# Four batch inputs of an attention: expert outputs weighted, summed and transposed in one TensorE product

## The chip, the cores and the metric

The kernel runs on one NeuronCore of one Trainium2 chip. Its time is the device time of one launch in microseconds (us), the median of several runs. The engines of a core run their own instruction queues side by side and wait for one another by semaphores: TensorE (PE in the profile), VectorE (DVE), ScalarE (ACT), GpSimd (POOL), and SyncE (SP), which here only issues transfers. ACTq, POOLq and SPq are the transfers that an engine issues.

## The reference

Two layers on x of 4 sequences x 512 tokens x 512 channels. Every sublayer reads its input through a gate (`cond`), a bidirectional recurrence that gives one factor per token and channel, which is multiplied with a sigmoid of x. The first layer is a Mamba-2 block and a mixture of eight experts, the second a causal attention with 16 heads in 4 groups and a gated feed-forward. What the change touches is the end of the experts and the beginning of the attention:

```python
for e in range(E):                       # 8 experts, each token routed to 2
    h = x @ w1[e].T + b1[e]
    y = x_glu * sigmoid(1.702 * x_glu) * (x_lin + 1.0)
    ye = y @ w2[e].T + b2[e]
    we = sum(routing * (top_idx == e))
    out = out + ye * we[:, None]
x = x + out                              # end of the expert sublayer
u = sigmoid(x) * gate                    # input of the attention
k, v, q = u @ w_kv, u @ w_q              # then softmax(q k) v @ w_dense, added to x
```

## The kernel before

Everything is kept transposed: XT holds the 512 channels as 4 chunks of 128 partitions, and the 2048 tokens in the free dimension. Each engine's program is written out by hand in its own block, in the order in which it is to run; nothing is scheduled by a planner. A tensor that TensorE multiplies in the attention is split into a rounded part (`_hi`, a ScalarE copy) and the remainder (`_lo`, a VectorE subtraction), and each product is done as three (`three`, L341 to L343).

The experts run over 39 blocks of 128 gathered tokens. Their results go to `y_dram`, one row per token and chosen expert. After the last block, each batch (sequence) b of 4 has to be brought home. It has 4 blocks of 128 tokens (tb; a = 4b + tb counts all 16):

1. GpSimd (`gather_out`) issues two indirect transfers for a block, one per chosen expert, into `og` (two slots, reused) or, for blocks 2 and 3 of batch 0, into `og2`. From block 4 on, it first waits until the slot's former block has been transposed (`cb_T`).
2. VectorE (`weighted`) multiplies the first by its weight `we`, one number per token and so per partition, and adds the second times its own (`cb_sum`).
3. TensorE (`combine_T`) transposes the sum in 4 pieces into the PSUM bank `CB`.
4. VectorE (`combine`) adds the bank to XT (`cb_done`). There is one bank, so a transpose waits for the add before it.
5. `gated_input` makes the attention's input of the batch in four whole steps of 4 x 512 columns: a tanh on ScalarE, times the gate on VectorE, `u_hi` on ScalarE, `u_lo` on VectorE (`u_split`).

The attention goes over 16 items i (group x batch), with 4 heads h each. TensorE computes in turn keys, query, scores, transposed probabilities, context and the dense product of the item before. Batch 0 is brought home before item 0 (`batch_T(0)`, `batch_input(0)`), batch 1 in the middle of item 0 after the context of head 0, batch 2 at the end of item 0, batch 3 at the end of item 1. ScalarE's `k_hi_copy(0)` also waits for a transfer, because `k_hi` lies where the gate stage has its last values: `act.wait_ge(g_out[LATE], ...)`, the store of the last gate pair to `g_dram` by SyncE (`g_store`, L400). SyncE's queue in this stage is, in order: the gate of batch 0 (`u_g`), the attention weights' first part, a wait for `cb_sum` of 4 blocks, the other two parts, the gates of batches 1 to 3, this store. ScalarE's `att_hi` and VectorE's `att_lo` split the weights. GpSimd ends the last gate pair (`gate_result`, L512 to L516) between the gathers of batch 0 and those of batch 1.

## Time and profile before

| | |
|---|---|
| median of 3 runs | 2657.7 us (2654.98 to 2658.51) |
| profiled execution, its own time | 2656.02 us |
| its span in the profile | 2654.3 us |
| TensorE busy | 2254.9 us, 85% |
| VectorE busy | 1921.7 us, 72% |
| ScalarE busy | 933.3 us, 35% |
| GpSimd busy | 682.5 us, 26% |
| mean TensorE clock granted | 0.93 of full speed |

The times below count from the span's start. The experts' last result is stored at 1327 us, the first of the four batches is added at about 1349 to 1356 us, the last at 1537 us. A row of a timeline gives start, duration, engine, line of the kernel, operation, what it writes and reads, how many such in a row, and in brackets how long the engine stood idle before and what released it. The chain of waits is followed back from the last instruction. A share of busy time is an average over stages with different limits, so the stage is read by its own rows.

### The profile page before, as it was taken

Reading aid. Unit: us, or ns where it says so; the run is one execution under the profiler, and the core shown is the slowest. Engines: PE = TensorE matmul, PEld = TensorE weight load, DVE = VectorE, ACT = ScalarE, POOL = GpSimd, SP = SyncE. Lnnn points to the kernel's source line nnn. Section 1 sums busy time; section 2 is a strip of 40 time slices with the busy share of each in tenths; the row PEclk is TensorE's granted clock in tenths of the full one; section 3 lists DMA queues with packets and bytes.
Section 4 is the critical chain, followed back from the end, with each engine's and each line's share of the span. In section 5 each row is a group of like instructions: output and inputs, shape, how many; then the busy total and the mean of one; then the engine's idle time right before and its main releaser. Section 6 shows DMA issues by size and latency. Waiting matters only on the chain.

```text
span 2654.3 us, 32921 instructions
## 1 busy us (share of the span) xinstructions
PE 2254.9 (85%) x10143; PEld 1698.7 (64%) x10160; DVE 1921.7 (72%) x2901; ACT 933.3 (35%) x1910; POOL 682.5 (26%) x545
## 2 busy tenths in 40 slices
PE   0788979978885699988846889999999998999998
PEld 0344444443445578767635777887887877788886
DVE  8898888889885865666645557787787776566665
ACT  2252342342432232333322334444444444322222
POOL 5433434334341434333221002212212210000000
PEclk9899989989985899989967889999999999899999
DMA  5000001001023332343141000001001101000001
GB/s 200 16 32 32 32 16 48 16 25 39 32 79 125 136 112 65 111 150 111 48 162 41 24 16 32 32 0 40 32 0 40 48 16 57 31 24 24 24 12 63
DMA packets 50501, 142.17 MB, mean 54 GB/s; under 512 B 4768, under 2 KB 4768, under 8 KB 46064
## 3 DMA queue, kind: packets, MB, share of 16 engines
q1 hardware_dynamic: 31872, 89.89, 9.5%
q10 hardware_dynamic: 12864, 32.81, 3.3%
q0 software_dynamic: 5680, 18.62, 2.4%
q14 instruction: 65, 0.53, 0.1%
q8 instruction: 20, 0.33, 0.1%
HBM read 106.95 MB, written 34.34 MB: 53 GB/s over the span
## 4 chain that ended last, share of the span: by engine, by line
PE 42%; issue 29%; POOL 9%; DVE 9%; POOLq 5%; ACT 3%; DMA 1%; ACTq 1%; SPq 0%; DVEq 0%
PE bank L341 9%; PE bank L342 9%; PE bank L343 9%; PE bank L2211 4%; PE bank L2212 4%; PE bank L2213 4%; PE bank L2174 3%; POOLq L491 2%; POOL g_v L492 2%; POOL g_v L499 2%; POOLq L517 1%; DVE mw L1716 1%; PE bank L2206 1%; POOLq L514 1%; POOLq L503 1%
## 5 line engine op out<-in xcount | busy, mean ns | idle before, releaser
L2048 PE MATMUL bank<-um,w_in 128*128 128x512 f32 x576 | 260.6, 606 | 7.3 <-DVE lm L1440 7.1
L2048 PEld LDWEIGHTS bank<-um,w_in 128*128 128x128 f32 x576 | 108.9, 194 | 137.2 <-issue 125.7
L341 PE MATMUL bank<-u_hi,aw_hi 128*128 (+1 forms) x384 | 158.7, 413 | 9.4 <-issue 9.4
L1077 ACT ACTIVATE probs<-bank,nmx 128x128 f32<-128x128 f32 (+3 forms) x256 | 131.8, 528 | 90.8 <-DVE nmx L1837 90.8
L343 PE MATMUL bank<-u_hi,aw_lo 128*128 (+1 forms) x384 | 152.3, 397 | 0.0
L342 PE MATMUL bank<-u_lo,aw_hi 128*128 (+1 forms) x384 | 152.2, 396 | 0.0
L1084 ACT ACTIVATE pt_hi<-bank 128x512 fp32r<-128x512 f32 (+1 forms) x192 | 93.9, 526 | 161.1 <-PE bank L2174 161.1
L341 PE MATMUL bank<-u_hi,fw_hi 128*128 128x512 f32 x352 | 136.9, 389 | 0.0
L342 PE MATMUL bank<-u_lo,fw_hi 128*128 128x512 f32 x352 | 136.9, 389 | 0.0
L343 PE MATMUL bank<-u_hi,fw_lo 128*128 128x512 f32 x352 | 136.9, 389 | 0.0
L2174 PE MATMUL bank<-ident,probs 128*128 128x128 f32 x640 | 97.1, 285 | 46.3 <-DVE pt_lo L1852 26.4
L446 DVE TENSOR_TENSOR_SCAN g_s<-decay,g_s 128x512 f32<-128x512 f32 x96 | 127.7, 1371 | 5.0 <-POOL g_v L492 5.0
L1834 DVE TENSOR_REDUCE rinv<-bank 128x1 f32<-128x128 f32 (+3 forms) x256 | 107.6, 482 | 31.0 <-PE bank L2312 31.0
L498 POOL TENSOR_TENSOR g_eu<-g_eu,g_s 128x512 f32<-128x512 f32 x48 | 65.5, 1365 | 247.7 <-DVE g_s L459 247.7
L1852 DVE TENSOR_TENSOR pt_lo<-bank,pt_hi 128x512 fp32r<-128x512 f32 (+1 forms) x192 | 108.4, 592 | 26.7 <-ACT pt_hi L1084 26.7
L2211 PE MATMUL bank<-mw,bu_hi 128*128 (+1 forms) x312 | 126.9, 407 | 0.0
L2212 PE MATMUL bank<-mw,bu_hi 128*128 (+1 forms) x312 | 126.2, 404 | 0.0
L2213 PE MATMUL bank<-mw,bu_lo 128*128 (+1 forms) x312 | 126.1, 404 | 0.0
L1996 DVE SCALAR_TENSOR_TENSOR XT<-bank,cols,XT 128x512 f32<-128x512 f32 x176 | 120.0, 743 | 3.4 <-PE bank L343 3.4
L2174 PEld LDWEIGHTS bank<-ident,probs 128*128 128x128 f32 x640 | 75.8, 146 | 60.0 <-DVE probs L1846 23.1
L459 DVE TENSOR_TENSOR_SCAN g_s<-decay,g_s 128x512 f32<-128x512 f32 x96 | 112.3, 1211 | 1.7
L2148 PE MATMUL bank<-lm,xdt 128*64 128x128 f32 x512 | 68.3, 343 | 53.2 <-DVE xa L1540 51.9
(380 smaller groups left out, 6238.4 us busy)
## 6 DMA issues: line engine op xcount, KB each, us to landing
m_stage<-in_moe SPq DMA_DIRECT2D x21, 1024.0 KB, 6.3
y_slot<-m_o ACTq DMA_DIRECT2D x39, 256.0 KB, 2.5
g_v<-in_fT SPq DMA_DIRECT2D x18, 512.0 KB, 3.4
gates<-g_v SPq DMA_DIRECT2D x18, 512.0 KB, 2.8
f_stage<-in_ffn SPq DMA_DIRECT2D x11, 768.0 KB, 4.4
u_g<-gates SPq DMA_DIRECT2D x8, 1024.0 KB, 5.6
aw_in<-in_att SPq DMA_DIRECT2D x4, 1280.0 KB, 6.2
w_in<-in_w_in ACTq DMA_DIRECT2D x1, 4640.0 KB, 16.8
```

Source lines behind the costliest of these rows:

```text
L341: nc.tensor.matmul(out, hi_w, hi_x, start=start, stop=False)
L342: nc.tensor.matmul(out, hi_w, lo_x, start=False, stop=False)
L343: return nc.tensor.matmul(out, lo_w, hi_x, start=False, stop=stop)
L446: nc.vector.tensor_tensor_scan(x, d, x, 0.0, ALU.mult, ALU.add).then_inc(g_vec, 1)
L459: nc.vector.tensor_tensor_scan(x[:, ::-1], d, x[:, ::-1], 0.0, ALU.mult, ALU.add).then_inc(g_vec, 1)
L1077: A(probs[:, h % 2, PR_AT[qb]:PR_AT[qb] + w], S_[bk][:, c0:c0 + w], ACT.Exp, bias=nmx[:, h % 2, qb:qb + 1], scale=SCALE, accum_out=rsum[:, ...
L1996: V.scalar_tensor_tensor(xm, FD[m][:], col("down_s", m), xm, ALU.mult, ALU.add).then_inc(fx_acc, 1)
L2048: mm = M(dst[:], w_in[:, k, c0:c0 + P], um[:, k, :], start=(k == 0), stop=(k == KC - 1))
L2174: return nc.tensor.transpose(out, src, ident[0:dim, 0:dim])
L2211: M(out, x_hi[:, kc, :], hi, start=False, stop=False)
L2212: M(out, x_hi[:, kc, :], lo, start=False, stop=False)
L2213: mm = M(out, x_lo[:, kc, :], hi, start=False, stop=(kc == KC - 1))
```

## The change

- `og` has four slots and `og2` is gone. A gather of block a waits only for the block four before it (`cb_T` at a - 3).
- ScalarE writes for each block two diagonal matrices, `w_diag` = identity times the weight of the partition's token (`spread_weights`), 8 instructions of 128x128 per batch. The four calls stand at the beginning, after the first input, and after the inputs of batches 1 and 2.
- TensorE multiplies the gathered rows by the diagonals: `og[:, tb, k]` as weights, `w_diag` as moving operand, both experts into the same PSUM piece. This weights, sums and transposes. It takes 8 products per block in place of 4 transposes, and uses two PSUM banks in turn. It waits for the gathers and for `w_spread`.
- VectorE's `weighted` is gone.
- The first input is made in four parts, one per channel chunk (`first_input`), and keys of item 0 start part by part.
- SyncE waits for `cb_T` of 4 blocks instead of `cb_sum`.

Of the diff's hunks only the changed lines stand here; line numbers of the new code are those of its own file.

```diff
@@ -231,7 +231,7 @@
-                    og = sb("og", [P, 2, 2, C], F32, s3)
+                    og = sb("og", [P, TB, 2, C], F32, s3)
@@ -240,10 +240,9 @@
-                with ExitStack() as s3:
-                    og2 = sb("og2", [P, 2, 2, C], F32, s3)
+                w_diag = sb("w_diag", [P, TB, 2, P], F32, s2)
...
@@ -631,7 +626,7 @@
-                    sp.wait_ge(cb_sum, TB)
+                    sp.wait_ge(cb_T, TB)
@@ -776,12 +771,11 @@
-                    pool.wait_ge(cb_T, a - 3 if a < TB + 2 else a - 1)
-                dst = og2 if 2 <= a < TB else og
+                    pool.wait_ge(cb_T, a - TB + 1)
-                        dst[:, a % 2, k, :], None, y_dram,
-                        bass.IndirectOffsetOnAxis(ap=pos_i[:, k, a:a + 1], axis=0)).then_inc(og_in[a % 2], 16)
+                        og[:, a % TB, k, :], None, y_dram,
+                        bass.IndirectOffsetOnAxis(ap=pos_i[:, k, a:a + 1], axis=0)).then_inc(og_in[a % TB], 16)
@@ -1033,7 +1027,7 @@
-                k = (3 if ffn else 2) * BATCH + b - 1
+                k = (3 if ffn else 2) * BATCH + b - 1 + IN_PARTS
@@ -1042,6 +1036,31 @@
+            def first_input():
+                def tanh_part(c):
+                    A(u_in[:, c, tok(0)], XT[:, c, tok(0)], ACT.Tanh, scale=0.5).then_inc(x_tanh, 1)
+                def hi_part(c):
+                    act.wait_ge(u_ready, FIRST + 2 * BATCH + c)
+                    A(u_hi[:, c, tok(0)], u_in[:, c, tok(0)], ACT.Copy).then_inc(u_hi_ready, 1)
+                act.wait_ge(cb_done, TB)
+                act.wait_ge(masks_ready, N_MASKS)
+                tanh_part(0)
+                for c in range(1, KC):
+                    tanh_part(c)
+                    hi_part(c - 1)
+                hi_part(KC - 1)
+            def spread_weights(b):
+                if b:
+                    act.wait_ge(cb_T, TB * b)
+                for a in range(b * TB, (b + 1) * TB):
+                    for k in range(2):
+                        A(w_diag[:, a % TB, k, :], ident[:], ACT.Copy, scale=we[:, k, a:a + 1]).then_inc(w_spread, 1)
@@ -1087,8 +1106,10 @@
+            spread_weights(0)
-            gated_input(0)
+            first_input()
+            spread_weights(1)
@@ -1116,6 +1137,7 @@
+                    spread_weights(2)
@@ -1140,6 +1162,7 @@
+                    spread_weights(3)
@@ -1784,28 +1807,17 @@
-            def weighted(b, tb):
-                a, s_ = b * TB + tb, tb % 2
-                og = out_slot(b, tb)
-                dve.wait_ge(og_in[s_], 64 if b == 0 else 32 * (b * 2 + tb // 2 + 1))
-                V.tensor_scalar(og[:, s_, 0, :], og[:, s_, 0, :], we[:, 0, bass.ds(a % NT, 1)], None, ALU.mult).then_inc(cb_first, 1)
-                dve.wait_ge(cb_first, a + 1)
-                V.scalar_tensor_tensor(og[:, s_, 0, :], og[:, s_, 1, :], we[:, 1, bass.ds(a % NT, 1)], og[:, s_, 0, :], ALU.mult,
-                                       ALU.add).then_inc(cb_sum, 1)
-                V.tensor_tensor(xa_, xa_, CB[:].rearrange("p (k t) -> p k t", k=KC), ALU.add).then_inc(cb_done, 1)
+                V.tensor_tensor(xa_, xa_, TT_[tb % 2][:].rearrange("p (k t) -> p k t", k=KC), ALU.add).then_inc(cb_done, 1)
-                k = layer * BATCH + b - 1
+                k = layer * BATCH + b - 1 + IN_PARTS
@@ -1862,14 +1874,33 @@
+            def first_input():
+                def gate_part(c):
+                    u = u_in[:, c, tok(0)]
+                    dve.wait_ge(x_tanh, 2 * BATCH + c)
+                    V.scalar_tensor_tensor(u, u, 1.0, u_g[:, c, tok(0)], ALU.add, ALU.mult).then_inc(u_ready, 1)
+                def lo_part(c):
+                    dve.wait_ge(u_hi_ready, c + 1)
+                    V.tensor_tensor(u_lo[:, c, tok(0)], u_in[:, c, tok(0)], u_hi[:, c, tok(0)].bitcast(F32),
+                                    ALU.subtract).then_inc(u_split, 1)
+                dve.wait_ge(g_fetched[0], 32)
+                gate_part(0)
+                for c in range(1, KC):
+                    gate_part(c)
+                    lo_part(c - 1)
+                lo_part(KC - 1)
-                weighted(b, 0)
-                    if tb < TB - 1:
-                        weighted(b, tb + 1)
-                gated_input(b)
+                if b:
+                    gated_input(b)
+                else:
+                    first_input()
@@ -2263,24 +2294,28 @@
-                a, s_ = b * TB + tb, tb % 2
-                pe.wait_ge(cb_sum, a + 1)
-                if not (isinstance(a, int) and a == 0):
-                    pe.wait_ge(cb_done, a)
+                a = b * TB + tb
+                pe.wait_ge(og_in[tb], 32 * (b + 1))
+                pe.wait_ge(w_spread, 2 * (a + 1))
+                if a >= 2:
+                    pe.wait_ge(cb_done, a - 1)
-                    mm = transposed(CB[:, kc * P:(kc + 1) * P], out_slot(b, tb)[:, s_, 0, kc * P:(kc + 1) * P])
+                    o = slice(kc * P, (kc + 1) * P)
+                    for k in range(2):
+                        mm = M(TT_[tb % 2][:, o], og[:, tb, k, o], w_diag[:, tb, k, :], start=(k == 0), stop=(k == 1))
-            def project(dst, at, b):
+            def project(dst, at, b, by_part=False):
+                    if by_part:
+                        pe.wait_ge(u_split, kc + 1)
-                project(PP[KV_BANK], A_K, i % BATCH).then_inc(k_done, 1)
+                project(PP[KV_BANK], A_K, i % BATCH, isinstance(i, int) and i == 0).then_inc(k_done, 1)
@@ -2347,7 +2382,6 @@
-            pe.wait_ge(u_split, 1)
...
```

On TensorE, batch 0's blocks stand between the last expert product and the keys. Before:

```order
L2213 MATMUL bank<-mw,by_lo 128x512
L2174 MATMUL bank<-ident,og 128x128 [waits cb_sum]
L2174 MATMUL bank<-ident,og 128x128 x3
L2174 MATMUL bank<-ident,og 128x128 [waits cb_done,cb_sum]
L2174 MATMUL bank<-ident,og 128x128 x3
L2174 MATMUL bank<-ident,og 128x128 [waits cb_done,cb_sum]
L2174 MATMUL bank<-ident,og 128x128 x3
L2174 MATMUL bank<-ident,og 128x128 [waits cb_done,cb_sum]
L2174 MATMUL bank<-ident,og 128x128 x3
L341 MATMUL bank<-u_hi,aw_hi 128x512 [waits aw_split0,u_split,cb_done]
```

Now:

```order
L2244 MATMUL bank<-mw,by_lo 128x512
L2305 MATMUL bank<-w_diag,og 128x128 [waits w_spread,og_in0]
L2305 MATMUL bank<-w_diag,og 128x128 x7
L2305 MATMUL bank<-w_diag,og 128x128 [waits w_spread,og_in1]
L2305 MATMUL bank<-w_diag,og 128x128 x7
L2305 MATMUL bank<-w_diag,og 128x128 [waits cb_done,w_spread,og_in2]
L2305 MATMUL bank<-w_diag,og 128x128 x7
L2305 MATMUL bank<-w_diag,og 128x128 [waits cb_done,w_spread,og_in3]
L2305 MATMUL bank<-w_diag,og 128x128 x7
L340 MATMUL bank<-u_hi,aw_hi 128x512 [waits u_split,aw_split0,cb_done]
```

Each group of four transposes has become a group of eight products. The waits for VectorE's sum became waits for the gather and the diagonals, and only the third and fourth block wait for an add.

On ScalarE, from the attention weights' first copy to the keys' copy (`g_out2` is the semaphore of the gate store). Before:

```order
L1050 ACTIVATE aw_hi<-aw_in 128x2560 [waits a_staged0]
L1041 ACTIVATE u_in<-XT 128x4x512 [waits cb_done]
L1044 ACTIVATE u_hi<-u_in 128x4x512 [waits masks_ready,u_ready]
L1056 ACTIVATE k_hi<-bank 128x512 [waits k_done,g_out2]
L1068 ACTIVATE q_hi<-bank 128x512 [waits q_done] x2
```

Now:

```order
L1063 ACTIVATE w_diag<-ident,we 128x128 x8
L1069 ACTIVATE aw_hi<-aw_in 128x2560 [waits a_staged0]
L1043 ACTIVATE u_in<-XT 128x512 [waits masks_ready,cb_done]
L1043 ACTIVATE u_in<-XT 128x512
L1047 ACTIVATE u_hi<-u_in 128x512 [waits u_ready]
L1043 ACTIVATE u_in<-XT 128x512
L1047 ACTIVATE u_hi<-u_in 128x512 [waits u_ready]
L1043 ACTIVATE u_in<-XT 128x512
L1047 ACTIVATE u_hi<-u_in 128x512 [waits u_ready] x2
L1063 ACTIVATE w_diag<-ident,we 128x128 [waits cb_T]
L1063 ACTIVATE w_diag<-ident,we 128x128 x7
L1075 ACTIVATE k_hi<-bank 128x512 [waits k_done,g_out2]
```

Eight diagonals precede the copy of the attention weights; tanh and `u_hi` have become four parts each; eight more diagonals stand ahead of `k_hi`.

In the middle of item 0, ScalarE's queue from the context of head 0 to the probabilities of head 1. Before:

```order
L1088 ACTIVATE cx_hi<-bank 128x512 [waits c_done]
L1041 ACTIVATE u_in<-XT 128x4x512 [waits cb_done]
L1044 ACTIVATE u_hi<-u_in 128x4x512 [waits masks_ready,u_ready]
L1084 ACTIVATE pt_hi<-bank 128x512 [waits t_done] x2
L1084 ACTIVATE pt_hi<-bank 128x256 [waits t_done]
```

Now:

```order
L1107 ACTIVATE cx_hi<-bank 128x512 [waits c_done]
L1035 ACTIVATE u_in<-XT 128x4x512 [waits cb_done]
L1038 ACTIVATE u_hi<-u_in 128x4x512 [waits masks_ready,u_ready]
L1063 ACTIVATE w_diag<-ident,we 128x128 [waits cb_T]
L1063 ACTIVATE w_diag<-ident,we 128x128 x7
L1103 ACTIVATE pt_hi<-bank 128x512 [waits t_done] x2
L1103 ACTIVATE pt_hi<-bank 128x256 [waits t_done]
```

The third set of diagonals stands between `u_hi` and `pt_hi`. The fourth stands in the same way after the `u_hi` of batch 2, ahead of `vT`.

## Rows read from the trace of the kernel before

**Rows 1.** The page's part 4: shares of the chain that ended last.
```profile
PE 42%; issue 29%; POOL 9%; DVE 9%; POOLq 5%; ACT 3%; DMA 1%; ACTq 1%; SPq 0%; DVEq 0%
```

**Rows 2.** The chain of waits, 1300 to 1480 us: start us, us, what.
```profile
1355.53 8.62 issue
...
1404.67 3.89 DMA og<-y_slot,pos_i
```

**Rows 3.** TensorE's timeline: start us, us, engine, line, operation; in brackets the idle time before.
```profile
1364.15 0.77 PE L341 MATMUL bank<-u_hi,aw_hi 128*128 128x512 f32 x1 [9.36 <-issue]
...
1369.37 0.40 PE L341 MATMUL bank<-u_hi,aw_hi 128*128 128x512 f32 x1
...
1374.82 0.39 PE L341 MATMUL bank<-k_hi,q_hi 128*128 128x512 f32 x1
...
1393.73 0.79 PE L341 MATMUL bank<-pt_hi,v_hi 128*128 128x512 f32 x1 [2.79 <-DVE v_lo L1822]
...
1396.88 0.27 PE L343 MATMUL bank<-pt_hi,v_lo 128*128 128x128 f32 x1
...
1453.04 0.39 PE L343 MATMUL bank<-u_hi,aw_lo 128*128 128x512 f32 x1
...
1524.03 0.39 PE L343 MATMUL bank<-u_hi,aw_lo 128*128 x1
```

**Rows 4.** VectorE's timeline, 1344 to 1540 us.
```profile
1344.60 1.48 DVE L1793 TENSOR_SCALAR og<-og,we 128x512 f32<-128x512 f32 x1
...
1347.67 0.47 DVE L1793 TENSOR_SCALAR og<-og,we 128x512 f32<-128x512 f32 x1
...
1354.83 0.69 DVE L1802 TENSOR_TENSOR XT<-XT,bank 128x512 f32<-128x512 f32 x1 [1.27 <-PE bank L2174]
...
1411.73 0.69 DVE L1802 TENSOR_TENSOR XT<-XT,bank 128x512 f32<-128x512 f32 x1 [1.27 <-PE bank L2174]
...
1420.88 1.28 DVE L1852 TENSOR_TENSOR pt_lo<-bank,pt_hi 128x512 fp32r<-128x512 f32 x2
...
1465.96 0.69 DVE L1802 TENSOR_TENSOR XT<-XT,bank 128x512 f32<-128x512 f32 x1 [1.27 <-PE bank L2174]
...
1536.91 0.69 DVE L1802 TENSOR_TENSOR XT<-XT,bank 128x512 f32<-128x512 f32 x1 [1.27 <-PE bank L2174]
```

**Rows 5.** ScalarE's timeline, 1365 to 1420 us.
```profile
1369.92 0.60 ACT L1056 ACTIVATE k_hi<-bank 128x512 fp32r<-128x512 f32 x1 [8.19 <-DMA gates<-g_v]
...
1418.54 1.07 ACT L1084 ACTIVATE pt_hi<-bank 128x512 fp32r<-128x512 f32 x2
```

**Rows 6.** ScalarE's instructions grouped by line: xcount, busy us, mean ns, idle before.
```profile
L928 ACT ACTIVATE bank<-bank,dt 128x128 f32<-128x128 f32 x256 | 68.6, 354 | 57.1 <-PE bank L2117 56.8
```

**Rows 7.** GpSimd's timeline, 1343 to 1350 us.
```profile
1343.44 2.36 POOL L515 TENSOR_TENSOR g_v<-g_v,g_s 128x512 f32<-128x512 f32 x1 [1.45 <-issue]
...
1349.19 0.99 POOL L782 DMA_INDIRECT og<-y_slot,pos_i  x1 [2.00 <-PE bank L2174]
```

**Rows 8.** SyncE's timeline of issues, 1350 to 1380 us.
```profile
1352.81 0.80 SPq L628 DMA_DIRECT2D aw_in<-in_att  x2
```

**Rows 9.** DMA in 1350 to 1375 us: all packets; issues by line, KB each, median us to landing.
```profile
DMA packets 2465, 6.05 MB, mean 242 GB/s; under 512 B 160, under 2 KB 160, under 8 KB 2336
...
gates<-g_v SPq DMA_DIRECT2D x1, 512.0 KB, 14.3
...
og<-y_slot,pos_i POOLq DMA_INDIRECT x4, 4.0
```

**Rows 10.** TensorE's timeline, 350 to 365 us (Mamba stage).
```profile
354.49 0.94 PE L2151 MATMUL bank<-cT,state 128*128 128x128 f32 x6
...
361.03 1.56 PE L2151 MATMUL bank<-cT,state 128*128 128x128 f32 x6
```

**Rows 11.** Busy us of each engine by stretch, PEclk, DMA share, GB/s.
```profile
1355.00:1370.00 15.00, 5.85 (x15) 4.67 (x16) 5.10 (x3) 3.90 (x3) 0.00 (x0) 0.52 0.93 351
1445.00:1453.00 8.00, 8.00 (x45) 6.93 (x45) 5.03 (x14) 3.62 (x11) 0.00 (x0) 1.00 0.00 0
```

More of the change, by code:

```diff
@@ L298, in network @@
             sem("y_ready"), sem("ty_done"), sem("by_hi_ready"), sem("y_split"), sem("dn_done"), sem("out_copied"))
-        og_in = [sem(f"og_in{i}") for i in range(2)]
-        cb_first, cb_sum, cb_T, cb_done = sem("cb_first"), sem("cb_sum"), sem("cb_T"), sem("cb_done")
+        og_in = [sem(f"og_in{i}") for i in range(TB)]
+        w_spread, cb_T, cb_done = sem("w_spread"), sem("cb_T"), sem("cb_done")
         a_staged, aw_hi_ready, aw_split = ([sem(f"{n}{i}") for i in range(3)] for n in ("a_staged", "aw_hi_ready", "aw_split"))
@@ L329, in network @@
         UG, UL, DN, TP = bank[0:3], bank[3:6], bank[6], bank[7]
-        CB = bank[4]
+        IN_PARTS = 3
         S_, TT_, PP = bank[0:3], bank[3:5], bank[5:8]
@@ L400, in g_store @@
             eng.dma_start(dst, g_values(s)).then_inc(g_out[min(s, LATE)], 16)
-        def out_slot(b, tb):
-            return og2 if b == 0 and tb >= 2 else og
         def att_lo(eng, ops, n, part):
@@ L2393, in att_pe @@
                     if first:
-                        pe.wait_ge(u_split, 2)
+                        pe.wait_ge(u_split, 2 + IN_PARTS)
                     else:
                         with pe.If(i < BATCH - 1):
-                            pe.wait_ge(u_split, i + 2)
+                            pe.wait_ge(u_split, i + (2 + IN_PARTS))
                     pe.wait_ge(c_split, HPG * i + 1)
@@ L2447, in ffn_up @@
                 if par == 0:
-                    pe.wait_ge(u_split, BATCH + b + 1)
+                    pe.wait_ge(u_split, IN_PARTS + BATCH + b + 1)
                 if not (isinstance(s, int) and s == 0 and b < 2):
```

## The prediction

> **What bounds the kernel now.** I read the page first, then the chain of waits between 1300 and 1480 us, then each engine's timeline around the four places where expert outputs are added to XT, last the DMA view of that stretch. On the page TensorE is the largest engine of the chain, but 29% of it is "issue" [rows 1], so the question is where TensorE stands still. The change touches one stage only, the four batch inputs of the attention. In the chain they are visible: for batch 1 (and in the same way for batch 2) it runs through a gather and its landing, 3.89 us, and for batch 0 through 8.62 us in which TensorE waits for the first input [rows 2]. In batch 1 TensorE has its last attention product at 1396.88 (ends 1397.15) and VectorE ends the last add at 1412.42; in batch 2 it is 1453.43 to 1466.65, in batch 3 1524.42 to 1537.60 [rows 3, 4]. In each the first two blocks go through at once, and the third waits for a gather that could not start before its slot was free [rows 2].
>
> Batch 0 is bound in another way. After the last add (1355.52) the input runs as whole pieces, and keys begin at 1364.15; query 0 follows them at 1369.37. But k_hi, the copy of the keys' result, starts at 1369.92, and the profile puts its wait down to a DMA, the store of the last gate pair [rows 3, 5]. That store is the last on SyncE's queue and lands 14.3 us after its issue [rows 9], which puts the issue at 1355.6. So the store is a second wall, within 0.4 us of the keys' end. With it five more loads are sent after the wait for the fourth block, from 1352.81 on [rows 8]. Of the 6.05 MB that move in 1350 to 1375, four gathers of 0.26 MB (128 x 512 x 4 bytes) are GpSimd's and the other 5.0 MB are this queue's [rows 9].
>
> **The change, part by part.** *Price of one product.* The trace has the same kind of product (128x128 fp32 weights that change each time, 128 moving columns) in the Mamba stage, 3 of them as 6 records, once at each of the two levels of the clock (2.4 and 1.2 GHz). At the high one they take 0.94 us, less a last record of 0.27: 0.134 us per record, 0.267 per product. At the low one 1.56, less 0.42: 0.228 per record, 0.456 per product [rows 10]. A block is 8 products, 2.14 or 3.65 us, in place of 4 transposes. A batch is 32: 8.5 or 14.6 us. What goes away is VectorE's scaling (0.47 us a block undisturbed [rows 4]) and its weighted sum, and, in batches 1 to 3, the wait for the late gathers. The gathers of batch b+1 now start when the blocks of batch b are done, some 40 us ahead. TensorE's new waits, for a block's gathers and its two diagonals, have everything else of TensorE queued behind them, but both are met long before in batches 1 to 3. GpSimd's waits moved with its gathers; behind them stand only gate products that begin after batch 3. PSUM alternates between two banks, so that the add of 0.69 us hides beside the next block's products; one add and a hop of 0.15 remain at the end: 0.84 us.
>
> *Batch 2.* TensorE is at the high clock when it arrives (PEclk 1.00 in 1445 to 1453 [rows 11]) and now goes on without a gap: 1453.43 + 8.5 + 0.84 = 1462.8 against 1466.65: -3.9 us. *Batch 3* alike: 1524.42 + 9.3 = 1533.8 against 1537.60: -3.8 us.
>
> *Batch 1.* TensorE comes in at the low clock: its context product starts at 1393.73 after 2.79 us of idle time. Elsewhere the clock came back after about 5 us of unbroken products (keys from 1364.15, 12 products in 5.2 us, 0.43 each, until the first of query 0 at 1369.37 takes 0.40 us where the first of keys took 0.77; query 0 and 1, 24 products, then take 5.45, 0.23 each, until 1374.82 [rows 3]). With no gap before the new products it would be back at about 1398.9. Then 8 of the 64 records go at 0.228 and 56 at 0.134: 9.3 us, so 1397.15 + 9.3 + 0.84 = 1407.3 against 1412.42: -5.1 us. If the clock stays low it is 1412.6: +0.2. I take -5.1, since fp32 products of this kind do run at the high clock in rows 10, and keep +0.2 for the range.
>
> *Diagonal weights.* Eight ScalarE copies of 128x128 per batch. No row has one from SBUF; the nearest is the exp of a 128x128 tile, whose 256 take 68.6 us: 0.268 us apart, 2.15 us for eight [rows 6]. From below they cost nothing, where another wait covers them; from above the 0.354 us of a single one, 2.8 us for eight. The first eight fall into ScalarE's wait for aw_in, which ends with the weights' copy just before VectorE's split, the second into its 8.19 us wait for the store: nothing. The third stand between u_hi and pt_hi of head 1. There pt_hi started at 1418.54 and pt_lo at 1420.88, because u_lo held VectorE [rows 4, 5]; now the first pt_hi ends at 1418.54 + 2.15 + 0.60 = 1421.3, so pt_lo is 0.5 us late. The fourth stand before vT as well, one more copy of 0.6 us that overlaps a little: 0.9 us. Together +1.4 (0 to 2.7).
>
> *Batch 0.* The first two blocks need only gathers that have landed by then (VectorE's scaling at 1344.60, which waits for two of them, follows the split with no idle time [rows 4]), and run while VectorE splits weights until 1344.6. The third needs the first add. VectorE's first scaling at this place took 1.48 us, the second 0.47; meanwhile GpSimd was at work, 2.36 us on one instruction [rows 4, 7]. So I let the first add (0.69) take 1 us more as well, to 1346.3. Two blocks follow, at the low clock for 5 us and then at the high one: 22 records of 0.228 and 10 of 0.134, until 1352.6 (1350.6 all high, 1353.6 all low). SyncE is released by the fourth block, which is where it was before, at 1352.8 [rows 8]. So the last add ends about 1353.5, 2 us earlier. In four parts, with a tanh or copy of 0.6 and an add of 0.69 us each, VectorE needs 8 x 0.6 and the first tanh: all of u_lo at about 1359.7, the keys end at 1361.2. That is 8 us earlier than before, and it is worth nothing if the store lands at 1369.9. The store lands later still. GpSimd issues a gather each 1.25 us, and now eight of them instead of four, from 1347.2 on instead of 1349.19 (it had waited 2.00 us for the first block). With 4.0 us from issue to landing, two of them were still under way at 1355 before, and four are now. The 0.52 MB more, at the 351 GB/s of 1355 to 1370, are 1.5 us: the store lands at 1371.4 [rows 7, 9, 11]. From there k_hi and k_lo (0.6 and 0.69 us) to 1372.7. Query 0 is done by then, but TensorE has stood for some 8 us, so that query 1 runs at the low clock, 12 x 0.43 = 5.1 us, until 1377.8. Before, scores began at 1374.82 [rows 3]. Batch 0 is +3.0 us. Bounds: -0.5 (store at 1369.0, clock back halfway) to +4.
>
> *Sum.* +3.0 - 5.1 - 3.9 - 3.8 + 1.4 = -8.4 us. The profiled execution took 2656.02 us, 1.7 more than its span; it becomes 2647.6. The median of the runs, 2657.7, is 1.7 above it and becomes 2649.3. Attention after batch 3 and the feed-forward part keep their rows.
>
> One rule of the Trainium skill bears on batch 0. Its page "SBUF — State Buffer", section "Who interferes with whom", says that a VectorE instruction with at most one SBUF input, outside the two-port modes, does not contend with GpSimd. The trace agrees that the scaling, an SBUF to SBUF operation, was slow beside GpSimd; no row shows an add from PSUM there. By the page the first add would take 0.69 us, the two blocks and the store would be 0.9 us earlier, and the total would be 2648.4.
>
> **Rivals.** *The clock stays low in batch 1*, all else as forecast: 2649.3 + 5.3 = 2654.6. For it: this stretch began low, after idle time [rows 3]. Against: the products now join the context product with no gap. *The wall comes earlier.* If the first blocks run at the high clock, SyncE is released 2 us earlier and batch 0 is +0.9: 2647.2. The whole gain of the four parts (k_hi at 1361.3 instead of 1369.92, -8.6 in place of +3.0: 2637.7) would want the store to land 9 us earlier, which 5.0 MB behind that release can't do. *Slower:* the products cost more than the gathers' wait. It is one mechanism, TensorE at the low clock through all blocks. Batches 2 and 3 end at 1453.43 + 14.6 + 0.84 = 1468.9 and 1539.9, +2.2 us each; batch 1 is +0.2, batch 0 +3.8 (0.8 us later release), with ScalarE's 1.4: +9.8, 2667.5. It decides from (1466.65 - 0.84 - 1453.43) / 32 = 0.387 us per product, between the 0.267 and the 0.456 of the two levels. For it: the products are short and many. Against: rows 10 has such products at the high clock. *The gathers are not ready*, so that the third block waits as before: 2657. Against it speak the 40 us of lead.
>
> **How the numbers follow.** Forecast 0.58; low clock in batch 1 0.17; earlier wall 0.12; the whole first-input gain 0.03; low clock in all batches 0.07; gathers late 0.03. The range takes in the bounds of batch 0, of the clock in batch 1 and of ScalarE's copies: from 2657.7 - 0.5 - 5.1 - 7.7 + 0.6 = 2645 to 2657.7 + 4 + 0.2 - 7.7 + 2.7 = 2657, and a little below for the earlier wall: 2643 to 2657. Within 0.2% means 5.3 us, about what a measurement of this kernel tells from no change, so faster means under 2652.4. That is the forecast nearly whole (0.55), the earlier wall and the whole gain (0.15): 0.70. Same: the low clock in batch 1, the late gathers and the rest of the forecast, 0.23. Slower 0.07.
>
> **What would show it.** Rows of w_diag and og on TensorE with 0.13 us between records in batches 2 and 3 and no idle time ahead of them; 9 us from the last values product to the last add. k_hi of batch 0 still released by the gates store, at 1370 to 1372, and keys ended by 1362. TensorE's wait before query 1 of 6 us or more, and low-clock products behind it. GpSimd's gathers of a batch all issued within the batch before. pt_lo of batch 1 released by ScalarE's pt_hi and not by u_lo. The prediction is wrong if the store lands near 1361, if a w_diag record takes 0.19 us or more at the high clock, or if any og gather ends a wait in batches 1 to 3.

## The result and the profile after

The changed kernel takes 2644.4 us (median of 6 runs, 2638.8 to 2651.3), the one before beside it 2658.1 (6 runs). The ratio is 0.995, its 95% interval 0.9938 to 0.9963: 13.7 us, 0.5%, faster. 2649.3 was forecast. The profiled execution took 2644.21 us (span 2642.5), against 2656.02. Below, three executions (one each of the kernels with the whole input, with late gathers and without the product) were in a slower state, 2796 to 3330 us, and are left out of the medians.

Two profiles of this kernel can't be laid over each other by the clock on the wall. The Mamba and expert stages, which are the same code, end at another moment in each launch: the last expert result is sent (`y_slot<-m_o` on ScalarE's queue) at 1326.86 us in the profile of before and at 1331.96 in that of after, and between 1326.9 and 1335.5 in all the profiles of this case. So every time below that is compared is counted from this transfer, called "from y".

On the page, TensorE's part of the chain and its "issue" are nearly as before [rows 1]:

```profile
PE 43%; issue 29%; POOL 9%; DVE 8%; POOLq 5%; ACT 3%; DMA 2%; ACTq 1%; SPq 0%; DVEq 0%
```

TensorE's timeline after (start us, us, engine, line, operation; in brackets the idle time before and who ended it) answers to [rows 3]:

```profile
1344.30 10.35 PE L2305 MATMUL bank<-w_diag,og 128*128 128x128 f32 x64 [13.01 <-DMA og<-y_slot,pos_i]
1358.37 0.77 PE L340 MATMUL bank<-u_hi,aw_hi 128*128 128x512 f32 x1 [3.72 <-DVE u_lo L1886]
...
1377.70 0.79 PE L340 MATMUL bank<-u_hi,aw_hi 128*128 128x512 f32 x1 [10.91 <-DVE k_lo L1830]
...
1382.19 0.39 PE L340 MATMUL bank<-k_hi,q_hi 128*128 128x512 f32 x1
...
1404.68 7.57 PE L2305 MATMUL bank<-w_diag,og 128*128 128x128 f32 x64
1413.03 1.09 PE L2205 MATMUL bank<-ident,probs 128*128 128x128 f32 x8 [0.78 <-DVE XT L1814]
...
1422.88 0.66 PE L2205 MATMUL bank<-ident,probs 128*128 128x128 f32 x2 [6.59 <-DVE pt_lo L1864]
...
1453.14 7.30 PE L2305 MATMUL bank<-w_diag,og 128*128 128x128 f32 x64
1461.22 1.09 PE L2205 MATMUL bank<-ident,probs 128*128 128x128 f32 x8 [0.78 <-DVE XT L1814]
...
1519.52 7.30 PE L2305 MATMUL bank<-w_diag,og 128*128 128x128 f32 x64
1527.93 1.09 PE L2205 MATMUL bank<-ident,probs 128*128 128x128 f32 x8 [1.10 <-DVE XT L1814]
```

A whole batch, 64 records, is one row without idle time ahead of it in batches 1 to 3. It takes 7.3 us at the high clock, 0.114 us per record. Batch 0's row begins as soon as its first gather has landed, beside VectorE's split of the weights. The 8 transposes behind each batch take 1.09 us; in the kernel before, where TensorE came out of idle time, they took 1.97 in batches 1 to 3. That alone saves nothing, since TensorE then waits for pt_lo in both kernels.

VectorE's last add of each batch answers to [rows 4]; ScalarE's k_hi, pt_hi and the new diagonals to [rows 5]; then two rows of GpSimd [rows 7] and SyncE's store [rows 8]:

```profile
1346.16 3.62 DVE L405 TENSOR_TENSOR aw_lo<-aw_in,aw_hi 128x2560 fp32r<-128x2560 f32 x1 [12.39 <-ACT aw_hi L1069]
1349.70 0.67 DVE L1814 TENSOR_TENSOR XT<-XT,bank 128x512 f32<-128x512 f32 x1
...
1354.69 0.69 DVE L1814 TENSOR_TENSOR XT<-XT,bank 128x512 f32<-128x512 f32 x1 [1.10 <-PE bank L2305]
...
1412.29 0.69 DVE L1814 TENSOR_TENSOR XT<-XT,bank 128x512 f32<-128x512 f32 x1 [1.10 <-PE bank L2305]
...
1422.05 1.29 DVE L1864 TENSOR_TENSOR pt_lo<-bank,pt_hi 128x512 fp32r<-128x512 f32 x2 [0.53 <-ACT pt_hi L1103]
...
1460.48 0.69 DVE L1814 TENSOR_TENSOR XT<-XT,bank 128x512 f32<-128x512 f32 x1 [1.10 <-PE bank L2305]
...
1526.86 0.69 DVE L1814 TENSOR_TENSOR XT<-XT,bank 128x512 f32<-128x512 f32 x1 [1.10 <-PE bank L2305]
...
1376.32 0.60 ACT L1075 ACTIVATE k_hi<-bank 128x512 fp32r<-128x512 f32 x1 [13.24 <-DMA gates<-g_v]
...
1419.10 2.43 ACT L1063 ACTIVATE w_diag<-ident,we 128x128 f32<-128x128 f32 x8
1421.44 1.05 ACT L1103 ACTIVATE pt_hi<-bank 128x512 fp32r<-128x512 f32 x2
...
1348.69 2.22 POOL L510 TENSOR_TENSOR g_v<-g_v,g_s 128x512 f32<-128x512 f32 x1 [1.60 <-issue]
...
1352.93 0.99 POOL L776 DMA_INDIRECT og<-y_slot,pos_i  x1 [0.80 <-PE bank L2305]
...
1354.68 0.80 SPq L623 DMA_DIRECT2D aw_in<-in_att  x2
...
1357.80 8.54 SPq L399 DMA_DIRECT2D gates<-g_v  x1
```

k_hi still waits for the store of the last gate pair, 13.24 us now. The DMA view of 1350 to 1375 us shows why (issues: KB each, median us to landing), against [rows 9]:

```profile
DMA packets 2775, 7.08 MB, mean 283 GB/s; under 512 B 223, under 2 KB 223, under 8 KB 2645
...
gates<-g_v SPq DMA_DIRECT2D x1, 512.0 KB, 18.5
...
og<-y_slot,pos_i POOLq DMA_INDIRECT x8, 7.1
```

The store is issued 2.9 us earlier than before (25.8 us from y against 28.7) and takes 18.5 us in place of 14.3. Eight gathers move beside it instead of four; two experiments below part the two effects. It lands 44.3 us from y, before 43.1. Scores begin 50.2 us from y, before 48.0. From y to the moment when TensorE goes on after batch 3 it is 204.8 us, before 219.9. That is 15.1 us, of which this pair of launches gives back 5.1 in the stages ahead and gains 1.8 in the rest of the run behind.

### The profile page after: what moved, and what is told of

Same layout as the page of the kernel before. It is cut to its first block, busy times and chain, and to the rows that moved or that the text cites. A ratio compares the mean times of both kernels' runs of the same rounds, so it can differ in the third digit from the quotient of the medians.

```text
span 2642.5 us, 33318 instructions
## 1 busy us (share of the span) xinstructions
PE 2266.7 (86%) x10335; PEld 1713.3 (65%) x10352; DVE 1902.3 (72%) x2875; ACT 943.0 (36%) x1948; POOL 684.0 (26%) x545
## 4 chain that ended last, share of the span: by engine, by line
PE 43%; issue 29%; POOL 9%; DVE 8%; POOLq 5%; ACT 3%; DMA 2%; ACTq 1%; SPq 0%; DVEq 0%
PE bank L340 9%; PE bank L341 9%; PE bank L342 9%; PE bank L2242 4%; PE bank L2243 4%; PE bank L2244 4%; PE bank L2205 3%; POOLq L486 2%; POOL g_v L487 2%; POOL g_v L494 2%; PE bank L2305 1%; POOLq L512 1%; DVE mw L1739 1%; PE bank L2237 1%; POOLq L509 1%
```

## Experiments

All times but the medians are from the profiled execution of each kernel. "Resumes" is TensorE's first operation that waits for pt_lo behind batch 3's input (1536.75 us in the profile of after). "The stop" is a delay in batches 1 and 2 that is told below.

| kernel | median us | last add of batch 0 ends, from y | scores begin, from y | TensorE resumes, from y |
|---|---|---|---|---|
| before | 2658.1 | 28.7 | 48.0 | 219.9 |
| before, early store | 2658.7 | 28.7 | 47.9 | 219.8 |
| before, four places only | 2644.8 | 28.6 | 50.0 | 206.1 |
| changed | 2644.4 | 23.4 | 50.2 | 204.8 |
| changed, second and third time | 2644.6, 2644.1 | 23.3, 23.1 | 49.8, 50.3 | 204.5, 205.6 |
| changed, late gathers | 2656.1 | 23.1 | 48.4 | 220.6 |
| changed, later diagonals | 2642.6 | 23.2 | 51.5 | 205.4 |
| changed, whole input | 2651.5 (with the stop) | 23.1 | 50.4 | 211.5 |
| changed, whole input, early store | 2644.7 (with the stop) | 23.1 | 41.8 | 204.6 |
| changed, early store, first time | 2641.3 (with the stop) | 23.1 | 37.2 | 198.9 |
| changed, early store, second time | 2632.5 | 23.3 | 37.2 | 191.8 |
| early store and later diagonals | 2629.1 | 23.3 | 37.2 | 188.6 |
| early store, no product | 2637.6 | 28.7 | 41.8 | 198.0 |

The experiments ran in three series, each on another chip (0, 12 and 8), with the kernel before beside them each time: its medians were 2659.3, 2657.3 and 2660.4 us. The first series holds the early store (first time), the whole input, both together, and the early store in the kernel before; the second the changed kernel again, four places only, late gathers and later diagonals; the third the rest.

**The store as the wall of batch 0.** The edit moves one line of SyncE's program:

```diff
                     att_load(0, 0)
+                    g_store(sp, G_ATT - 1, LATE)
                     sp.wait_ge(cb_T, TB)
...
-            g_store(sp, G_ATT - 1, LATE)
```

> The changed kernel, with one transfer moved on SyncE's queue: the store of the last gate pair is issued before the wait for the fourth block instead of behind it and behind five loads. Theory (the store is the wall of batch 0): in the changed kernel k_hi waits 13.2 us for it and starts at 1376.3, while the keys' last part is ready to start at about 1366. With the store landed by then, k_hi is freed by the keys at about 1369 to 1370 and query 1 follows query 0 without a stop and at the high clock. Scores then begin some 10 us after the start of the keys instead of 24: the stretch from the last m_o copy to TensorE's return after the fourth batch input shrinks from 205.4 us to 193 to 197, and the whole run is 8 to 12 us shorter than the changed kernel's. Rival A (something else holds k_hi or query 1 within a few us, such as VectorE's k_lo behind u_lo): less than 3 us. Rival B (TensorE stays at the low clock through this stretch anyway, since it begins after idle time): 3 to 7 us.

The whole input is the second edit (`gated_input(0)` in place of `first_input()`, keys wait for the whole `u_lo`), and both together the third:

> The changed kernel, with the first input made in one piece again, as before. Theory (the store is the wall, so the four parts bring nothing): keys end 8 us later, at about 1371, and k_hi still starts when the store lands at about 1376. Query 0 then runs close to k_hi, TensorE's stop before query 1 shrinks from 10.9 us to 3 or so, and query 1 may run at the high clock: 0 to 2.5 us shorter than the changed kernel in this stage. Rival (the four parts carry the gain, and the forecast had it by luck): 6 to 8 us longer.

> Both edits together: first input in one piece, store issued before the wait. With the two kernels above and the changed one it makes a square. Theory: here no store holds k_hi, and the four parts are missing, so this one is 6 to 8 us longer than the kernel with the early store alone, although the same edit cost nothing while the store was the wall. Against the changed kernel it is 3 to 5 us shorter. Rival (the two are independent): the difference between whole and four parts is the same in both rows of the square.

> The kernel before, with the store alone moved ahead of the wait. There the keys' end and the store's landing were 0.4 us apart. Theory: less than 1 us, not to be told from the kernel before; k_hi is now released by TensorE instead of the transfer. Rival (the store's place was the real cost of the stage already): 3 us or more.

In the stage itself the wall theory held. k_hi of the four kernels (changed with early store, with whole input, with both; before with early store), each from its ScalarE timeline:

```profile
1365.58 0.60 ACT L1075 ACTIVATE k_hi<-bank 128x512 fp32r<-128x512 f32 x1 [0.89 <-issue]
```

```profile
1376.05 0.60 ACT L1075 ACTIVATE k_hi<-bank 128x512 fp32r<-128x512 f32 x1 [12.97 <-DMA gates<-g_v]
```

```profile
1370.91 0.60 ACT L1075 ACTIVATE k_hi<-bank 128x512 fp32r<-128x512 f32 x1 [4.93 <-PE bank L342]
```

```profile
1371.90 0.60 ACT L1056 ACTIVATE k_hi<-bank 128x512 fp32r<-128x512 f32 x1 [7.79 <-PE bank L343]
```

With the early store, nothing of the DMA holds k_hi, and scores begin 37.2 us from y, 13.0 earlier than in the changed kernel. With the store in its place, whole input and four parts are alike (50.4 and 50.2); with it early, the four parts are worth 4.6 us (41.8 against 37.2), and 3.4 in the medians, where 6 to 8 were expected. In the kernel before, the early store is worth nothing: 0.9997, 0.9988 to 1.0007. The two walls there stood 0.4 us apart.

The whole times did not fit: 2641.3, 2651.5 and 2644.7 us, where 2632 to 2636, 2642 to 2644 and 2639 to 2641 were expected. In the totals, with the whole input 7 us above the changed kernel, the rival by which the four parts carry 6 to 8 us seemed right. The timelines show 6 to 7 us lost in a place that no edit touches. VectorE's adds of batch 1, a gather of GpSimd and TensorE behind them, in the kernel with the early store:

```profile
1397.34 0.69 DVE L1814 TENSOR_TENSOR XT<-XT,bank 128x512 f32<-128x512 f32 x1 [1.10 <-PE bank L2305]
1399.13 0.69 DVE L1814 TENSOR_TENSOR XT<-XT,bank 128x512 f32<-128x512 f32 x1 [1.10 <-issue]
1404.39 0.69 DVE L1814 TENSOR_TENSOR XT<-XT,bank 128x512 f32<-128x512 f32 x1 [4.58 <-remote]
...
1402.07 0.95 POOL L776 DMA_INDIRECT og<-y_slot,pos_i  x1 [0.30 <-issue]
1404.63 0.95 POOL L776 DMA_INDIRECT og<-y_slot,pos_i  x1 [1.60 <-remote]
...
1393.52 7.36 PE L2305 MATMUL bank<-w_diag,og 128*128 128x128 f32 x64
1405.13 1.11 PE L2205 MATMUL bank<-ident,probs 128*128 128x128 f32 x4 [4.26 <-DVE XT L1814]
```

The fourth add should follow 1.79 us behind the third, at 1400.92. It starts 3.47 us later, GpSimd's seventh gather at the same moment, both put down to "remote"; both wait for the end of TensorE's fourth block, whose records end at 1400.88. Behind it TensorE is at the low clock (8 transposes in 1.97 us instead of 1.09). The same is there in batch 2 and in the two other kernels (2.8 to 3.5 us), and not in batch 3. So the changed kernel and the early store ran again, in two other series:

> The changed kernel once more, unaltered, beside the others. In the three kernels with an early store or a whole input, VectorE's fourth add in batches 1 and 2 starts 3.5 us later than TensorE's last product would let it, the seventh gather on GpSimd is released at the same moment, and both are put down to 'remote'. The first profile of the changed kernel has no such stop. Theory 1 (the stop comes and goes with the launch or the chip and has nothing to do with the edits): it is in this run too, twice, about 7 us, and the median is near 2651. Then the square reads: whole input +0, early store -10, both -7, as the wall says. Theory 2 (the stop belongs to those kernels and not to this one): none here, 2644.4 as before, and the square reads +7, -3, 0.

> The changed kernel a third time, in one series with the early store. Open is the 3.5 us stop at the fourth block of batches 1 and 2, which all three kernels with products of the first series had and no kernel of the second. Theory S (it goes with the series): here the changed kernel and the early store are alike, both with it (near 2651 and 2641) or both without it (2644 and 2634 to 2636). Theory K (it goes with the kernel): this one has none, 2644.

> The early store alone once more. Theory S: 8 to 12 us shorter than the changed kernel of this series. Theory K: the stop is there twice again, 2641, 3 us shorter, although scores begin 11 to 13 us earlier.

The changed kernel had no stop in any of its three profiles. The early store, the very same kernel, had it twice in its first profile and not at all in its second: 2632.5 us, 0.9893 of before (0.9878 to 0.9909). So theory S is right as against theory K: the same kernel has the stop in one series and not in another, so it does not follow from the edit. Since each series had its own chip, and the changed kernel itself did not run in the first, the record can't tell whether the stop belongs to that chip or to that time. (Between the two controls theory 2 had looked right; it rested on series that were not the same.) From y to the resumption it cost 7.0 us, 198.9 against 191.8. Without it the early store is worth 11.6 us in the series it shares with the changed kernel, within the 8 to 12 expected, and the square of the four kernels (changed; whole input; whole input and early store; early store) reads, from y to the resumption, 204.8, about 205, about 197.5 and 191.8. The two in the middle are estimates: 211.5 less the 6.3 us that its two stops are long, and 204.6 less 7. What the stop is, no run shows; the kernel before with the early store, which has no such blocks, was profiled in the first series without it.

Keys, k_hi and scores of the early store, second time, and the store's own line in its DMA view (1350 to 1375 us):

```profile
1357.03 0.76 PE L340 MATMUL bank<-u_hi,aw_hi 128*128 128x512 f32 x1 [3.71 <-DVE u_lo L1886]
...
1367.96 0.39 PE L340 MATMUL bank<-k_hi,q_hi 128*128 128x512 f32 x1
...
1362.58 0.60 ACT L1075 ACTIVATE k_hi<-bank 128x512 fp32r<-128x512 f32 x1 [0.90 <-PE bank L342]
```

```profile
gates<-g_v SPq DMA_DIRECT2D x1, 512.0 KB, 2.9
```

k_hi waits 0.90 us for the keys' last product and for nothing else. The same 0.5 MB land in 2.9 us ahead of the queue's other loads and in 18.5 behind them.

**Four places or the product.** First the kernel before with four places only:

```diff
-                    og = sb("og", [P, 2, 2, C], F32, s3)
+                    og = sb("og", [P, TB, 2, C], F32, s3)
...
-                    pool.wait_ge(cb_T, a - 3 if a < TB + 2 else a - 1)
+                    pool.wait_ge(cb_T, a - TB + 1)
```

> The kernel before with one part of the change alone: four gather places, so that the gathers of batch b+1 start during batch b. VectorE still weights and sums, TensorE still transposes, the first input is whole. Theory (in batches 1 to 3 the late gathers were the cost, and the product is worth little beyond): after the last product of the attention the first transpose follows 2.6 us later as before, the next three at 1.95 us, the last add ends after 10.3 us in place of 15.3, 13.2 and 13.2: -5, -2.9, -2.9 us, less 0 to 1 us for the store behind four gathers more: 9 to 11 us shorter than the kernel before. Rival (the product carries the gain): less than 3 us shorter.

2644.8 us, ratio 0.9952 (0.994 to 0.9964): the four places alone bring all that the whole change brings, 2644.6 in the same series. That is more than expected. In batches 2 and 3 VectorE's first weighting starts before TensorE's last product ahead of the blocks has ended, so that the first transposes follow after 0.9 us and not after the 2.6 of batch 1. TensorE in batch 2:

```profile
1459.96 0.66 PE L2166 MATMUL bank<-ident,og 128*128 128x128 f32 x4 [0.94 <-DVE og L1787]
1461.84 0.63 PE L2166 MATMUL bank<-ident,og 128*128 128x128 f32 x4 [1.22 <-DVE XT L1794]
1463.69 1.09 PE L2166 MATMUL bank<-ident,og 128*128 128x128 f32 x4 [1.22 <-DVE XT L1794]
1465.64 1.09 PE L2166 MATMUL bank<-ident,og 128*128 128x128 f32 x4 [0.87 <-DVE XT L1794]
```

The four groups of transposes follow at 1.9 us, and no gather ends a wait. From the end of the last product ahead of the blocks to the end of the last add it is 10.2, 8.4 and 8.4 us in the three batches, against 15.3, 13.2 and 13.2 before and 8.1, 7.9 and 7.9 with the product. So of the 17.8 us that the change takes out of these three stretches the places alone take 14.7 and the product 3.2, of which ScalarE's diagonals give back 1.7.

Then the changed kernel with gathers that wait as before (`pool.wait_ge(cb_T, a - 3 if a < TB + 2 else a - 1)`):

> The changed kernel, in which a gather waits as before for the block two before it, not four. Products with diagonals and the four parts stay. Theory (late gathers were the cost): block 3 of each batch waits for a gather that is issued after block 1: 1.8 + 2.5 + 4.0 us, block 4 for 2.5 more, then 1.8 + 0.7: 13.3 us from the context's last product to the last add where the changed kernel has 8.0. Three times 5.2 us, less up to 1 us in batch 0 (four gathers less ahead of the store): 14 to 16 us longer than the changed kernel, no better than the kernel before. Rival (the product carries the gain): up to 5 us longer.

2656.1 us, ratio 0.9997 (0.9988 to 1.0005), no better than before. In the stage it is 15.6 us longer than the changed kernel from y (mean of its three profiles), as expected; in the medians 11.5. Batch 2 on TensorE:

```profile
1455.10 3.73 PE L2305 MATMUL bank<-w_diag,og 128*128 128x128 f32 x32
1462.10 5.47 PE L2305 MATMUL bank<-w_diag,og 128*128 128x128 f32 x32 [3.27 <-DMA og<-y_slot,pos_i]
```

32 records in 3.73 us at the high clock, then 3.27 us of waiting for a gather, then 32 in 5.47 us, at a mean granted clock of 0.70. In batch 0, where only four gathers run beside the store, it scores 1.8 us earlier than the changed kernel.

These two kernels also part the store's landing. k_hi of the four places, then of the late gathers:

```profile
1381.28 0.60 ACT L1049 ACTIVATE k_hi<-bank 128x512 fp32r<-128x512 f32 x1 [10.98 <-DMA gates<-g_v]
```

```profile
1370.10 0.60 ACT L1075 ACTIVATE k_hi<-bank 128x512 fp32r<-128x512 f32 x1 [10.94 <-DMA gates<-g_v]
```

From y the store is issued at 28.7 and lands at 45.8 with eight gathers beside it (17.1 us); issued at 25.1 with four gathers it lands at 41.7 (16.6 us). Before, it was issued at 28.7 with four gathers and landed at 43.1; in the changed kernel at 25.8 with eight, and landed at 44.3. So four gathers more cost 2.7 us, and the earlier issue is worth some 1.4. These are single profiles.

**The diagonals' place.** In the changed kernel and in the one with the early store, `spread_weights(2)` and `(3)` move behind head 1's context copy:

```diff
                 ctx_hi(i, 1)
+                if first:
+                    spread_weights(2)
+                if mod == 1:
+                    spread_weights(3)
                 pt_hi_copy(i, 2)
```

> The changed kernel, with ScalarE's diagonals for batches 2 and 3 behind head 1's context copy instead of before pt_hi. Theory (they stand on the path, 0.6 us in batch 1 and 1.1 us in batch 2, since pt_lo now waits for pt_hi): those go and the eight copies, 2.43 us, fall in a wait of ScalarE: 1.7 us shorter. Rival 1 (no cover there either, the next pt_hi is late by as much): same. Rival 2: they now stand on a tighter place: up to 2.4 us longer.

> The changed kernel with the early store and the later diagonals of batches 2 and 3. The walls found so far are independent, so their prices add: 2 us less than the early store alone has in this series (0.6 us in batch 1, 1.1 us in batch 2). Rival: with the store gone, VectorE is the later one at the same place, and the diagonals' move is worth nothing: same as the early store alone.

2642.6 against 2644.6 and 2629.1 against 2632.5 us: 2.1 and 3.4, where 1.7 and 2 were expected. The intervals of the ratios overlap in both pairs, so the medians alone don't tell them apart; the rows do. From the last add's end to TensorE's return behind pt_lo the changed kernel took 9.9 us in batch 1 and 10.3 in batch 2; now it is 9.3 and 9.2, as in the kernel before. (From y the first kernel is no shorter, because scores begin 1.3 us later in that launch. The second is 3.2 shorter: 1.7 by these rows, and 1.3 because the clock came back sooner behind batch 1, which differs between launches of one kernel too, as told below.) ScalarE's timeline of the combined kernel shows the eight copies in a wait, with 0.29 us of it left over:

```profile
1414.00 2.44 ACT L1063 ACTIVATE w_diag<-ident,we 128x128 f32<-128x128 f32 x8
1416.73 1.09 ACT L1103 ACTIVATE pt_hi<-bank 128x512 fp32r<-128x512 f32 x2 [0.29 <-PE bank L2207]
```

It has the lowest median of all, 0.9885 of before (0.987 to 0.99) and 15 us below the changed kernel.

**Is the product worth nothing?** The early store with VectorE's weighting and TensorE's transposes back in place (`weighted`, no `w_diag`). With it come the single bank `CB`, so that a transpose waits for the add before it, and SyncE's wait for `cb_sum`; all that is priced together:

> The changed kernel with the early store, but VectorE weights and sums and TensorE transposes, as before the change: four gather places, four parts, no diagonals. Theory (the product is worth 1 us): batches 1 to 3 take 10.2, 8.4 and 8.4 us from the context's last product to the last add in place of 8.3, 8.0 and 8.0 (2.7 us more), and ScalarE's 1.7 us of diagonals are gone: 1 us longer than the early store alone without the stop of 3.5 us, and 6 us shorter than it with the stop, since kernels that transpose have not shown it. Rival (the product carries more, in batch 0, where its first two blocks run beside VectorE's split): batch 0's last add ends 2 us later here and scores too: 3 us longer in all.

2637.6 us, 5.0 more than with the product, and 6.1 from y to the resumption: both expectations were too low. The place is mainly batch 0:

```profile
1354.13 1.12 PE L2205 MATMUL bank<-ident,og 128*128 128x128 f32 x4 [21.60 <-DVE og L1804]
1356.12 1.09 PE L2205 MATMUL bank<-ident,og 128*128 128x128 f32 x4 [0.87 <-DVE XT L1811]
...
1360.03 1.09 PE L2205 MATMUL bank<-ident,og 128*128 128x128 f32 x4 [0.87 <-DVE XT L1811]
1364.85 0.77 PE L340 MATMUL bank<-u_hi,aw_hi 128*128 128x512 f32 x1 [3.73 <-DVE u_lo L1883]
```

Here TensorE stands 21.60 us (before: 21.61), until VectorE has split the weights (3.60 us) and weighted the first block (3.1 us); with the product it starts at the first gather. The last add ends 5.4 us later, scores begin 4.6 later. With the store as the wall, these microseconds were hidden, and the product seemed to bring nothing.

## Why the prediction came out right

The direction, the mechanism in batches 1 to 3 and the wall in batch 0 were right; the forecast was 4.9 us too careful in the median and 6.7 in the stage. In batch 0 part of the agreement is luck.

- *Batch 0, forecast +3.0, measured +2.3.* The store as the wall and TensorE's stop before query 1 (10.91 us, some 8 forecast) came as forecast, and so did the landing, within 0.2 us (1376.3 less the 5.1 us of the stages ahead: 1371.2, forecast 1371.4). The low clock behind the stop lasted 8 of the 12 products and not all. But two terms under the landing were off and cancelled. "The last add ends about 1353.5, 2 us earlier" was 5.2 earlier: the first add took 0.67 us and not 1 us more than 0.69, and from its end the two blocks behind it took 4.3 us and not 6.3, at a granted clock of 0.99. So SyncE came to the store's issue 2.9 us earlier, where the forecast had it released no earlier than before, and that was worth some 1.4 us. And the gathers beside the store cost 2.7 us by the same comparison, where "the 0.52 MB more ... are 1.5 us" had been taken: four gathers more are 1.05 MB.
- The page "SBUF — State Buffer" of the Trainium skill, section "Who interferes with whom", says that a VectorE instruction with at most one SBUF input, outside the two-port modes, does not contend with GpSimd; this add is one, since its other input is in PSUM. Here the trace agrees: 0.67 us, beside a GpSimd instruction of 2.22 us. The total that the prediction worked out by it, 2648.4, would have been 0.9 us closer.
- *Batches 1 to 3, forecast -5.1, -3.9, -3.8, measured -7.2, -5.4, -5.3.* The mechanism was right. The term that was mis-sized is the price of a record: 0.134 us, read from a row of six, against 0.114 in a row of 64. 32 products cost 7.3 us and not 8.5. In batch 1 the whole row took 7.57 (granted clock 0.97), so TensorE was back at the high clock within the first records and not after 8.
- *Between the batches, not in the forecast: -1.3.* Nearly all of it lies behind batch 1's pt_lo. TensorE reaches head 1's first context product 4.27 us after it resumes, before 5.58: the clock came back after 5 of the 12 products between and not behind them all. That is no gain of the change. The changed kernel took 4.27, 4.28 and 5.58 us there in its three profiles. The product in question, before (TensorE resumed at 1421.70) and after (1422.88):

```profile
1427.28 0.42 PE L341 MATMUL bank<-pt_hi,v_hi 128*128 128x512 f32 x1
```

```profile
1427.15 0.39 PE L340 MATMUL bank<-pt_hi,v_hi 128*128 128x512 f32 x1
```

- *Diagonals, forecast +1.4, measured +1.7* (0.6 and 1.1): eight copies in 2.43 us, 0.30 each, where 0.268 had been taken from an exp.
- The stage sums to -15.1 us against the -8.4 of the forecast, and the medians to -13.7. The rest is how far launches differ.
- Of the rivals, the early release came true, at 0.7 us under the forecast for batch 0 instead of 2.1; low clock in batch 1, low clock in all, and late gathers are refuted by the rows above. The whole gain of the four parts needs what the rival said, the store out of the way. With it scores begin 13.0 us earlier than in the changed kernel, where the rival had 11.6 against the forecast.
- What the prediction did not ask is which part of the change does the work. It took the product in place of weighting and transposes, and the end of the wait for late gathers, as one sum. The runs give 14.7 of the 17.8 us in batches 1 to 3 to the gathers' places, and the whole of the shorter time in the medians.

## What to carry over

When a stage has two walls close together, price each edit with the other wall standing and with it gone: here the four parts were worth 0 or 4.6 us (to the start of scores), the product 0 or 5.0 (medians; the 0 is read for product and four parts together), one moved store 0 or 11.6 (medians). If a change has several parts, run the cheapest alone: here a deeper buffer, which lets a transfer start a stage earlier, gave as much as the whole change. And put a small store that somebody waits for ahead of the bulk loads on its queue.

## What the runs showed of the hardware

- The same kernel in two series, on two chips, differed by 8.7 us (2641.3 and 2632.5). Its two profiles differ by two stops of 3.5 us, each with a lower clock behind it, 7.0 us in all. Only a control in the same series tells such a stop from an effect of the edit.
- 128x128 fp32 products whose weights change with every record run at 0.114 us per record in a long row at the high clock (7.30 us for 64), and at 0.17 where they start after idle time (5.47 for 32, mean granted clock 0.70).
- A store of 0.5 MB takes 2.9 us with an empty queue before it and 18.5 behind 4.5 MB of its own queue and beside eight gathers.
- After a wait of 6.6 us, TensorE got the high clock back after 5 of 12 products in two launches of one kernel and only behind all 12 in a third, which took 1.3 us more.
